# First-layer tiles grouped by feature half in the second pass of a two-layer decoder

## The reference

```
lt   = x[:, 1:17, :]                                  # 16 tokens
even, odd = lt[:, ::2], lt[:, 1::2]
m1 = (even[:, :4, :, None] * odd[:, :4, None, :]).reshape(B, 1024, 256)
m2 = (even[:, 4:, :, None] * odd[:, 4:, None, :]).reshape(B, 256, 1024)
h  = x @ W1.T + scale * einsum('bsd,bhd->bsh', x, m1) + b1
h  = gelu(h)
out = h @ W2.T + scale * einsum('bsh,boh->bso', h, m2) + b2
```

## The kernel before

| engine | last steps | first steps |
|---|---|---|
| PE | 1:tp, 1:g, 3:woa, 2:wqa, 1:hid0, 3:tp2 | 0:tp, 2:scores, 3:query projection |
| DVE | 1:1, 1:2, 1:3, 3:9 | 0:0, 3:10, 2:6, 0:1 |
| POOL | 1:0, 1:1 | 3:3, 0:0 |
| SP | 0:4, 1:0 | 0:0, 2:1, 3:1 |

## Time and profile before

### The profile page before, as it was taken

One profiled execution on the slowest core, in us unless ns is written; L12 is line 12 of the kernel. 1 busy time (PEld: TensorE's weight loads), 2 busy tenths in 40 slices (PEclk: granted clock), 3 DMA queues, 4 the chain that ended last, 5 costly groups with the idle time before them and its releaser, 6 DMA issues. The chain is left out here.

```text
span 3894.4 us, 81102 instructions
## 1 busy us (share of the span) xinstructions
PE 3612.2 (93%) x32871; PEld 2736.2 (70%) x32871; DVE 1980.3 (51%) x5378; ACT 1434.1 (37%) x3167; POOL 371.6 (10%) x455
## 2 busy tenths in 40 slices
PE   6999999999699898989898989994899999999997
PEld 4777777777576666666666666662788887878886
DVE  3665656566235353535353534452455555556554
ACT  2343344334134233333333343432344443444443
POOL 1111111111000000000000000000011111111111
PEclk9999999999699999999999999997899999999999
DMA  2000000000200001010101010001300001110000
GB/s 76 12 12 13 14 12 12 14 14 8 88 11 13 24 11 25 9 27 9 28 5 31 1 35 1 25 1 54 129 16 12 11 17 50 54 52 12 15 12 8
DMA packets 63555, 94.55 MB, mean 24 GB/s; under 512 B 7762, under 2 KB 59602, under 8 KB 62146
## 3 DMA queue, kind: packets, MB, share of 16 engines
q1 hardware_dynamic: 55074, 83.41, 6.9%
q0 software_dynamic: 8224, 7.36, 1.7%
HBM read 72.07 MB, written 18.37 MB: 23 GB/s over the span
## 5 line engine op out<-in xcount | busy, mean ns | idle before, releaser
L1478 PE MATMUL bps<-BXT,Bwexp 128*128 128x112 f32 x3072 | 379.7, 282 | 6.2 <-DMA Bwexp<-in_we 3.6
L1478 PEld LDWEIGHTS bps<-BXT,Bwexp 128*128 128x128 f32 x3072 | 361.7, 195 | 22.1 <-issue 9.3
L1243 DVE CUSTOM_DVE_ANT_0 PON<-pps,PMR 112x375 f32<-112x375 f32 x512 | 259.7, 544 | 194.3 <-PE pps L967 192.9
L1096 ACT ACTIVATE PPT<-pps,mcol 125x896 f32<-125x896 f32 x192 | 192.4, 1007 | 204.6 <-PE pps L986 204.4
L1564 PE MATMUL bps<-Bwexp,BPT 128*112 128x256 f32 x1024 | 235.9, 380 | 0.0
L657 POOL TENSOR_TENSOR rstd<-var,nhalf 112x1 f32<-112x1 f32 (+1 forms) x96 | 148.3, 1545 | 838.6 <-DVE var L575 459.1
L967 PE MATMUL pps<-PKT,PQM 64*112 64x375 f32 x1024 | 211.1, 501 | 6.0 <-DVE Pmx L1243 4.0
L1276 POOL TENSOR_TENSOR Prstd<-Pvar,nhalf 112x1 f32<-112x1 f32 x128 | 70.1, 548 | 1517.9 <-DVE Pvar L1164 1517.9
L1618 ACT ACTIVATE BPT<-bps,Bwexp 128x112 f32<-128x112 f32 x512 | 139.1, 354 | 170.9 <-PE bps L1478 170.9
L1564 PEld LDWEIGHTS bps<-Bwexp,BPT 128*112 128x112 f32 x1024 | 174.5, 177 | 35.3
L986 PE MATMUL pps<-PQM,PKT 64*125 64x448 f32 x768 | 187.5, 567 | 0.0
(11 more groups left out here) (302 smaller groups left out, 7280.8 us busy)
## 6 DMA issues: line engine op xcount, KB each, us to landing
Bwexp<-in_we SPq DMA_DIRECT2D x7, 2304.0 KB, 17.0
PCX<-in_ctx SPq DMA_DIRECT2D x32, 375.0 KB
BXIN<-xmid SPq DMA_DIRECT2D x64, 112.0 KB
out<-BY POOLq DMA_DIRECT2D x64, 112.0 KB, 2.9
Bwexp<-in_we SPq DMA_DIRECT2D x7, 777.0 KB, 4.6
wa_sb<-in_wa SPq DMA_DIRECT2D x1, 4736.0 KB, 14.8
Brexp<-in_re SPq DMA_DIRECT2D x7, 672.0 KB
XIN<-in_x SPq DMA_DIRECT2D x32, 112.0 KB
```

The lines of the kernel that those rows point to most:

```text
L1096: A(PT[s][0:KP, k, :, :].rearrange("p (i v) q -> p i (v q)", i=2), PS[s][0:KP, :, 0:QW], ACT.Exp, bias=mcol[:, k, bass.ds(at.n[s] + s * qu ...
L1243: m = v.tensor_tensor_reduce(out=ON[s][0:T, i * LC:(i + 1) * LC], in0=bank[s][i][0:T, 0:LC], in1=MR[s][:, :], scale=1.0, scalar=-3.0e38, o ...
L1478: m = mm(o[:, j * T:(j + 1) * T], wt[:, c, n0 + j * 128:n0 + (j + 1) * 128], rhs[:, c, :], start=(c == 0), stop=(c == 1))
```

## The change

The tiles of the first layer are dealt to the two banks by their feature half: bank g now holds tiles g, g+2, g+4 and g+6 instead of 4g to 4g+3. The four low-rank products of a bank then share one operand, half g of XN, and become one product of 448 columns. Its operands have 96 rows instead of 32; rows 32 to 95 of GS are zero by the mask from `ident`, and rows of XN are there anyway. For that PE makes the token products with 96 columns of weights, and DVE makes GS on 96 partitions. The gelu and the second layer follow the new tile order. All five tables of the second pass are new.

```diff
-            GS, G2 = [OS[s][0:32, :, :] for s in LANES], [OT[s][:, 0, :] for s in LANES]
+            GS, G2 = [OS[s][0:96, :, :] for s in LANES], [OT[s][:, 0, :] for s in LANES]
...
-                                mm(bank[s][g][:, j * T:(j + 1) * T], f1[:, c, (4 * g + j) * 128:(4 * g + j + 1) * 128], XT[s][:, c, :],
+                                mm(bank[s][g][:, j * T:(j + 1) * T], f1[:, c, (2 * j + g) * 128:(2 * j + g + 1) * 128], XT[s][:, c, :],
...
-                        for j in range(4):
-                            mt = 4 * g + j
-                            m = mm(bank[s][g][:, j * T:(j + 1) * T], XN[s][0:32, (mt % 2) * 128:(mt % 2) * 128 + 128], GS[s][:, mt // 2, :],
-                                   start=False, stop=True, skip_group_check=True)
+                        m = mm(bank[s][g][:, 0:QW], XN[s][0:96, g * 128:(g + 1) * 128], GS[s][:, :, :], start=False, stop=True, skip_group_check=True)
...
-                        mm(b1[0:32, 64:64 + T], XT[s][:, c, 1:33], XT[s][:, c, :], start=(c == 0), stop=(c == 1), skip_group_check=True)
+                        mm(b1[0:96, 64:64 + T], XT[s][:, c, 1:97], XT[s][:, c, :], start=(c == 0), stop=(c == 1), skip_group_check=True)
...
-                        m = mm(b1[rows[j], 0:64], ident[0:T, 9:73:2], XN[s][:, j:D:4], start=(j > 0), stop=True, skip_group_check=True)
+                        m = mm(b1[rows[j], 0:64], ident[0:T, 9:73:2], XN[s][:, j:D:4], start=(j == 3), stop=True, skip_group_check=True)
...
-                    second(range(0, 4))
+                    second(range(0, FT, 2))
...
-                    second(range(4, 8))
+                    second(range(1, FT, 2))
...
-                            mt = 4 * g + j
+                            mt = 2 * j + g
...
-                    v.scalar_tensor_tensor(out=GS[s], in0=b1[0:32, 64:64 + T].unsqueeze(1).to_broadcast((32, 4, T)),
-                                           scalar=cc("scale")[0:32, :], in1=ident[0:32, 1:9:2].unsqueeze(2).to_broadcast((32, 4, T)),
+                    v.scalar_tensor_tensor(out=GS[s], in0=b1[0:96, 64:64 + T].unsqueeze(1).to_broadcast((96, 4, T)),
+                                           scalar=cc("scale")[0:96, :], in1=ident[0:96, 1:9:2].unsqueeze(2).to_broadcast((96, 4, T)),
```

Of the tables, SP's whole and the two rows of DVE that move a step over the edge (lanes 1 and 3; step 3 of lane 1 and step 10 of lane 3):

```diff
-    "sp2": ((0, 338, 771, 771, 786,),
-            (0, 286, 485, 487, 556,),
-            (0, 311, 563, 563, 563,),
-            (67, 574, 574, 574, 578,)),
+    "sp2": ((0, 0, 221, 221, 221,),
+            (5, 180, 180, 188, 193,),
+            (6, 307, 307, 331, 341,),
+            (61, 415, 415, 415, 415,)),
...
-             (0, 58, 63, 63, 283, 287, 372, 375, 427, 540, 540, 566, 572, 624, 633, 633, 633, 672, 692, 750, 983, 984, 984,),
+             (13, 61, 63, 130, 248, 257, 376, 380, 429, 542, 542, 568, 585, 623, 635, 635, 635, 664, 698, 750, 943, 986, 986,),
...
-             (0, 0, 7, 31, 147, 147, 324, 332, 369, 412, 416, 440, 440, 538, 594, 594, 640, 667, 703, 767, 912, 976, 976,)),
+             (0, 0, 15, 15, 145, 221, 332, 332, 369, 412, 412, 436, 474, 541, 592, 595, 640, 664, 726, 765, 912, 972, 974,)),
```

## The result

The changed kernel takes 3803.64 us (median of four runs, 3800.48 to 3807.1) against 3894.14 us for the kernel before on the same chip (3891.59 to 3895.25): a ratio of 0.9772, 95% interval 0.976 to 0.9784. Its profiled execution took 3804.47 us, span 3802.8.

A forecast was written before the change was run, and what follows sets the result against it. The prediction took PE's own work to bound the kernel (busy 186.4 of 202.4 us a turn). Its terms, -20 + 3 - 34 - 3 + 4 = -50 us, took the profiled 3896.07 to 3846, forecast as 3845 us, range 3828 to 3871.

The forecast's parts named there:

- Products, -20 and +3: Second pass on PE: merged low-rank products save 20 us (6 to 26); token products with 96 columns cost 3 (0 to 6).
- 2:tp1, -3: PE in mid-turn: some 0.36 us of work moves into a 0.45 us wait before 1:g, saving 3 us over eight turns.
- New waits, +4: PE in mid-turn: swapped neighbouring steps may open short waits, 0.5 us per turn, 4 us in all (0 to 10).
- The edge of the loop, after: Second pass's loop edge: 0:tp starts 5.7 us earlier at each of six edges, 34 us saved (bounds 17 and 41).
- I take 4.5, near PE's row: DVE's jump at the loop's edge: 4.5 us without load traffic, between bounds of 3.36 (PE's) and 7.45 (DVE's then).
- PE's own jump no longer counts: PE at the loop's edge: its 3.4 us jump would end at 1524.8, before 0:tp is ready to start at 1526.2.
- The slow stretch behind the restart I leave as it is: PE's clock behind the loop's edge: granted 0.50 before as after an idle of over 5 us, so no gain counted.
- the long jump: Rival at the loop's edge: DVE's 7.45 us jump is its own, not the traffic's; edge gives 17, 3862 us; chance 0.20.
- the changes of form: Rival on PE's low-rank products: 96 rows still pay the switch between row counts, saving 6 not 20; 3859 us; chance 0.08.

The follow-up runs named there:

- sp_old_set1: The changed kernel with SP's table of before (loads back beside the edge) and one memset more ahead of DVE's loop (at 481): 3850.45 us, ratio 0.9878.
- after_set1: The changed kernel with one real memset of a column more ahead of DVE's loop, which then starts at 481: 3835.27 us, ratio 0.9852.
- code_only: The changed kernel with all old tables of the second pass, DVE's loop at 481: 3876.95 us, ratio 0.9961 to the kernel before.
- before_set110: The kernel before with 110 real memsets added ahead of DVE's loop, which then starts at 591: 3853.36 us, ratio 0.9893.
- order_only: The kernel before with all new tables of the second pass and nothing else, DVE's loop at 480: 3833.61 us, ratio 0.9852.
- four_96: The changed kernel with each 96-row low-rank product of 448 columns split into four of 112 columns: 3829.16 us, ratio 0.9838 to the kernel before.
- one_32: The changed kernel with its one low-rank product per bank reading only the first 32 of the 96 rows: 3830.13 us, ratio 0.9843.
- sp_old: The changed kernel with SP's table of before, which puts the loads back beside the edge, DVE's loop at 480: 3812.79 us, ratio 0.9787.

## Why the prediction missed

Differences between the medians, each step one thing more, split the 90 us: code 3894 to 3877, 17; the order of steps, all tables but SP's, to sp_old_set1 (3850), 27; the loads away from the edge, to after_set1 (3835), 15; the place by one instruction, to the changed kernel (3804), 31. By the ratios, which take each kernel against the kernel before on its own chip, the four are 15, 32, 10 and 31 us. The split holds in this sequence: in the old order the place alone was worth 41.

*Products, -20 and +3: right.* Forecast 0.89 us where full rows follow and 0.98 elsewhere; measured 0.88 and 0.97, with 0.112 us into the group. The Trainium skill (TensorEngine Tiling (Array Packing), Tiling Modes) has a drain at each change of mode and lists 32, 64 and 128 rows: the trace agrees, since 96 rows pay no change beside 128 and 32 rows pay 0.09 us at each side. Step g went from 0.73 to 0.90 us, (1486.67 - 1485.77), +0.17 in two thirds of the steps and +0.09 in the rest where +0.1 was taken: 4 us. Together -16, and code_only shows -17 (-15 by its ratio).

*2:tp1, -3:* in its place before 1:g it took 0.19 of the 0.45 us there (0.26 is left), 1.5 us over eight turns. *New waits, +4:* none; outside the edge PE's idle time per turn fell from 5.8 to 5.1 or 5.4 us.

*"The edge of the loop, after", -34: the step that failed.* Everything up to the jump came as worked out: 3:9 starts 1.16 us behind the start of the output projection (1.21 forecast), DVE reaches its jump 3.86 us behind it (3.91 forecast). Then:

- "I take 4.5, near PE's row", and a lower bound of 3.36. This took for granted that a jump always fetches. Given a fetch the length was well placed (4.2 us of idle time in after_set1 at 12 GB/s). But the loop moved from instruction 481 to 480 and there was no fetch: 0.45 us in place of 4.5. This is the 31 us.
- "PE's own jump no longer counts: 3:tp2 runs right behind 1:hid0 at 1521, and 1521.4 + 3.4 = 1524.8". Beside a stand of 4.5 us on DVE this bound decided nothing. Without it PE's jump does set the edge, and the bound was misplaced: by it PE could not have reached 0:tp before 1492.4 + 3.4 = 1495.8 in the changed kernel, and it did at 1494.06. The jump doesn't begin behind 3:tp2's products but when the last wait ahead of it ends. With XN ready at 1490.19, the first of q8's two packets comes 1.2 us later, at 1491.38, while PE still works off L835 and L839; 0:tp starts 2.7 us behind that packet. In before_set110 XN (L1170, 1515.53 to 1515.93) comes when these products are almost through, the packet at 1517.22, and 0:tp again 2.8 us behind it. In every kernel but the three with a fetch on DVE in the new order it is 2.6 to 3.1 us from PE's packet to 0:tp. The releaser that the row at 1494.06 names, DVE's XN, had landed at 1493.54, 0.5 us earlier (0.4 to 0.9 at the six edges); where XN really ends the wait, as in after_set1, 0:tp follows 0.05 us behind it. In order_only the profile puts three of these idle times down to "issue" instead, 1.7 us at most:

```profile
PE pps L816 <- issue: 4.8, 3, 1.7
```

- "The slow stretch behind the restart I leave as it is." In the kernel before the clock was at its lower level for 10 to 14 us at each of the six edges, from within the first idle time on; in after_set1, with idle times of 4.5 to 4.7 us, for 3.4 us at one edge and 6.8 at five; in the changed kernel at none.

From the output projection to 0:tp it is now 1494.06 - 1486.67 = 7.39 us, against 1531.91 - 1514.94 = 16.97; forecast was 11.26. That is 9.6 us per edge in place of 5.7, six times 58. The steps of the tables sum to 27 + 15 + 31 = 73. The 15 us between are mostly the slow stretches, 2.5 us an edge: in the kernel before PE is busy for 4.5 to 7.4 us of each, by estimate a loss of half of that. What the new order gives in mid-turn, 0.4 to 0.7 us of idle time a turn, is in them too. The forecast had 34.

Of the rivals, the long jump is refuted by after_set1, the changes of form by the rows of L839. None had "no fetch at all". A row that could have raised it was at hand, the 53 packets of q14 on the page of the kernel before, and the forecast doesn't use it. Its times would have shown three packets at each jump.

What stays open: why a loop at 481 or 609 is fetched again and one at 480 or 591 is not. The Trainium skill (Runtime: NRT & Kernel Launch, Instruction fetch mechanics) says that the memory of an engine is refilled in blocks of 16 KiB and that a branch out of the window fetches by DMA. That a jump may or may not fetch, by its place, agrees; but q14's packets are of 8 KB, and the two bad places lie 128 instructions apart, so for DVE the measured figure stands; q8's packets are all of 16 KB. Only four places were tried. Open too is the clock: four_96, order_only and one_32 fell to the lower level at six, four and three of the six edges, with idle times of 1.1 to 2.0 us, the repeat of the changed kernel and sp_old at two, and the changed kernel at none, with idle times of 1.2 to 1.7.

## What to carry to other kernels

Before pricing a wait "issue" behind a loop's jump, count the packets of that engine's instruction queue and where the loop starts in its program. A change that adds or drops a single instruction ahead of a loop can switch the fetch on or off, so give a loop edge a case in which the stand vanishes and one in which it appears, and try a few instructions of padding. Put no wait ahead of PE's jump that is released late: here the fetch began 1.2 us behind that release, and PE's next step came 2.6 to 3.1 us later, so by estimate products queued for some 4 us would hide it. And when a releaser named by the profile was done 0.5 us before the start that it is said to release, look for another.

## What the runs showed of the hardware

- DVE's loop of 355 instructions is fetched again on each jump when it starts at instruction 481 or 609, not at 480 or 591. A jump with a fetch leaves DVE idle for 4.1 to 4.3 us with light traffic, 5.9 to 6.4 with two sequences' loads in flight in the new order, and 7.0 to 7.9 in the old; without one, 0.45.
- The traffic delays the first packet of DVE's fetch (1.15 us behind its last step, or 2.8 to 4.6), and hardly what follows.
- PE fetches at each of its jumps. Alone that leaves it idle for 3.1 to 3.6 us; when the last wait ahead of the jump is released with 2.5 us of products still queued, for 1.2 to 1.7.
- After idle times of only 1 to 2 us the clock was granted at half in some turns of some kernels, for 3.4 to 6.8 us, and in others not.
